# Ends of the two transformer layers of a graph network rebuilt, with four new waits on the gather queue

## The reference, cut to what matters

```python
def transformer_conv(x, edge_index, Wq, bq, Wk, bk, Wv, bv, Ws, bs):   # H = 4 heads of C = 32
    q, k, v = (x @ Wq + bq), (x @ Wk + bk), (x @ Wv + bv)              # (N, H, C)
    alpha = einsum('ehc,ehc->eh', q[dst], k[src]) / sqrt(C)
    ealpha = exp(alpha - segment_max(alpha, dst)[dst])
    attn = ealpha / segment_sum(ealpha, dst)[dst]
    out = segment_sum(attn[..., None] * v[src], dst)
    return out.reshape(N, H * C) + x @ Ws + bs

h = relu(transformer_conv(x, edges, layer 1 weights))
out = transformer_conv(h, edges, layer 2 weights)
x = layernorm(x + out)
```

## Time and profile before

| | us |
|---|---|
| runs (3) | 3877.59, 3878.28, 3880.7; median 3878.28 |
| profiled execution, its own time | 3893.77 |
| its span, first to last instruction | 3892.1 |
| busy PE / DVE / POOL / ACT | 2947.8 / 2492.3 / 2423.7 / 1048.7 |
| mean granted TensorE clock | 0.829 of 2.4 GHz |

### The profile page before, as it was taken

One profiled execution on the slowest core, in us unless ns is written; L12 is line 12 of the kernel. 1 busy time (PEld: TensorE's weight loads), 2 busy tenths in 40 slices (PEclk: granted clock), 3 DMA queues, 4 the chain that ended last, 5 costly groups with the idle time before them and its releaser, 6 DMA issues. The chain is left out here.

```text
span 3892.1 us, 57650 instructions
## 1 busy us (share of the span) xinstructions
PE 2947.8 (76%) x14303; PEld 2002.8 (51%) x14345; DVE 2492.3 (64%) x8135; ACT 1048.7 (27%) x2557; POOL 2423.7 (62%) x2427
## 2 busy tenths in 40 slices
PE   6987997746666567999977999766677776676773
PEld 3455895534444433444435777643465564364663
DVE  8886553251111377999988888873567775384876
ACT  3730664110000043333315666620011120010211
POOL 2747777647777347777754666117777734777770
PEclk8975557568888788999988999888798898888986
DMA  2222222322222147888851222026787755687872
GB/s 70 68 60 52 62 62 58 48 61 53 53 53 53 29 90 197 239 236 236 241 138 57 68 70 70 22 78 181 196 243 223 226 167 139 182 245 194 252 238 65
DMA packets 397387, 493.91 MB, mean 127 GB/s; under 512 B 64035, under 2 KB 293992, under 8 KB 397138
## 3 DMA queue, kind: packets, MB, share of 16 engines
q0 software_dynamic: 92160, 244.83, 24.3%
q1 hardware_dynamic: 304978, 245.98, 21.8%
HBM read 376.23 MB, written 114.36 MB: 126 GB/s over the span
## 5 line engine op out<-in xcount | busy, mean ns | idle before, releaser
L1918 POOL DMA_INDIRECT got<-kv_table,pair_src x832 | 839.3, 1009 | 495.4 <-issue 249.3
L686 POOL DMA_INDIRECT y_got<-y_table,y_idx x416 | 399.7, 961 | 166.2 <-issue 126.4
L1164 POOL DMA_INDIRECT got<-t_table,tile_src x392 | 378.3, 965 | 175.4 <-issue 118.8
L2167 PE MATMUL psum<-acc 125*128 x1664 | 285.1, 324 | 219.0 <-DVE h L1984 195.1
L1313 PE MATMUL sums<-msg,hot 128*125 128x260 f32 x1664 | 394.0, 390 | 31.3 <-POOL msg L1255 28.6
L2167 PEld LDWEIGHTS psum<-acc 125*128 125x128 f32 x1664 | 243.7, 224 | 297.1 <-issue 295.8
L2179 PE MATMUL psum<-h,acc 128*128 128x128 f32 x1664 | 324.0, 329 | 68.1 <-ACT hot_b L2142 37.3
L1313 PEld LDWEIGHTS sums<-msg,hot 128*125 128x125 f32 x1664 | 305.9, 189 | 119.1 <-issue 72.3
L1984 DVE TENSOR_TENSOR h<-psum,got 128x512 f32<-128x512 f32 x208 | 143.4, 690 | 348.1 <-DMA got<-kv_table,pair_src 315.1
L1255 POOL TENSOR_TENSOR msg<-rows,msg 128x512 f32<-128x512 f32 x208 | 246.3, 1204 | 188.1 <-DVE msg L1281 148.7
L628 PE MATMUL psum<-zeros 128*128 128x512 bf16 (+1 forms) x946 | 340.6, 490 | 3.5 <-issue 2.4
(11 more groups left out here) (506 smaller groups left out, 5705.3 us busy)
## 6 DMA issues: line engine op xcount, KB each, us to landing
v_rows<-got SPq DMA_DIRECT2D x208, 256.0 KB, 3.4
small<-v_rows SPq DMA_DIRECT2D x208, 256.0 KB, 4.8
dst_row<-dst_rows SPq DMA_DIRECT2D x312, 128.0 KB, 4.8
rows<-x_rows SPq DMA_DIRECT2D x104, 256.0 KB
x_rows<-small SPq DMA_DIRECT2D x104, 128.0 KB, 3.6
x_rows<-got_w SPq DMA_DIRECT2D x104, 128.0 KB, 4.5
got<-kv_table,pair_src POOLq DMA_INDIRECT x832, 3.8
y_table<-y_stage SPq DMA_DIRECT2D x25, 448.0 KB
```

The source lines that it names most:

```text
L686: pool.indirect_dma_start(out=got[:, slot, j, :], out_offset=None, in_=y_table[:, :], in_offset=bass.IndirectOffsetOnAxis(ap=m.y_idx[:, co ...
L1164: pool.indirect_dma_start(out=got[:, col % ring, :], out_offset=None, in_=table[:, :], in_offset=bass.IndirectOffsetOnAxis(ap=m.tile_src[: ...
L1918: pool.indirect_dma_start(out=got[:, slot, j, :], out_offset=None, in_=kv_table[:, :], in_offset=bass.IndirectOffsetOnAxis(ap=m.pair_src[: ...
L2167: last = t.matmul(work[:, j * P:(j + 1) * P], hot_t[:, g % 2, j // 2, j % 2, :], m.acc[:, bass.ds(ws[j], 1), 0:D].rearrange("q o d -> q (o ...
```

## The change

In `conv_layer`: the parts are added to the sums in PSUM instead of in SBUF, and the division is one product that reads PSUM and writes `m.h`, in both layers. For n = 2 the skip path is added in seven joins, the positive part is taken by ACT when it copies the transposes out, and the transposes, products and joins alternate in groups of four windows (the alternation for n = 1 too); the input x of the residual is added by PE as a product with the identity into the PSUM of the second half's products. In the last chunk the one-hots of the first two groups are made in the softmax's waits, their messages come ahead of the share arithmetic, PE runs products with zeros during that softmax (4, 3 and 24) and none behind the groups. `conv_finish` only adds the skip path and norms. POOL gets a further wait in four loops.

```diff
@@ sort_edges, POOL
             for t in range(BY_DMA):
+                if 6 * t // 5 > 8:
+                    pool.wait_ge(placed, 6 * t // 5 - 8)
@@ relation_layer, POOL
                 if g >= SL:
                     pool.wait_ge(used, g - SL + 1)
+                elif g > 2:
+                    pool.wait_ge(counted, min(4 * g - 8, groups))
@@ gat_scores, POOL
                     pool.wait_ge(scored, (g - slots) // 2 + 1)
+                    pool.wait_ge(z_done, 4 * (g - 3))
@@ conv_layer, POOL
+                if g >= 7:
+                    pool.wait_ge(q_done, g - 6)
@@ conv_layer, DVE
+            def one_hots(s):
+                if s >= 2:
+                    dve.wait_ge(summed, s - 1)
+                v.tensor_tensor(hot[:, s % 2], ..., ALU.is_equal).then_inc(hot_ready, 1)
             def messages(s):
...
-                v.tensor_tensor(hot[:, s % 2], ..., ALU.is_equal).then_inc(hot_ready, 1)
+                if s not in groups_of(last_chunk)[0:2]:
+                    one_hots(s)
@@ softmax, DVE
                 dve.sem_inc(top_ready, 1)
+                if c == last_chunk:
+                    one_hots(p0 // G)
                 dve.wait_ge(high_ready, c + 1)
...
                 dve.sem_inc(high_read, 1)
+                if c == last_chunk:
+                    one_hots(p0 // G + 1)
                 dve.wait_ge(low_ready, c + 1)
@@
-            def finish_last():
-                (reciprocal, then by four windows: product, sum with the skip path, positive part)
+            def join(k):
+                h = m.h[:, 4 * k:ends[k], :]
+                v.tensor_tensor(h, h, m.acc[:, 4 * k:ends[k], 3 * D:4 * D], ALU.add).then_inc(joined, 1)
+            if n == 2:
+                for k in range(3):
+                    join(k)
+            for k in range(TG):
+                for w in range(4 * k, ends[k]):
+                    keep_node(w)
+                if n == 2 and k + 3 < TG:
+                    join(k + 3)
+            for w in range(W):
+                keep_node(W + w)
@@
+            for s in groups_of(last_chunk)[0:2]:
+                messages(s)
             (share arithmetic)
-            for s in groups_of(last_chunk):
+            for s in groups_of(last_chunk)[2:]:
                 messages(s)
+            border = [windows(nc, m.pair_win_i, ENG.DVE, CHUNK_AT[b + 1] - 1, 1)[0] for b in range(last_chunk)]
             dve.wait_ge(shares_ready, 1)
             dve.wait_ge(closed, 1)
...
-            go(v.tensor_copy(m.h[:, :, :].rearrange("q w d -> q (w d)"), psum[0:Q, 0:W * D]))
-            (copy of the denominators, adds in SBUF, sum over three)
+            dve.wait_ge(rejoined, 1)
+            link(v.tensor_copy(part[0:Q, :, :].rearrange("q b c -> q (b c)"), work[0:Q, 0:last_chunk * (D + 3 * H)]))
+            for b, w in enumerate(border):
+                sums, ws = psum[0:Q, bass.ds(w * D, D)], psum[0:Q, bass.ds(w * 3 * H + dens, 3 * H)]
+                go(v.tensor_tensor(sums, sums, part[0:Q, b, 0:D], ALU.add))
+                link(v.tensor_tensor(ws, ws, part[0:Q, b, D:D + 3 * H], ALU.add))
+            (sum over three, maximum with 1e-30, reciprocal, all into inv)
+            v.tensor_tensor(m.h[...], psum[0:Q, 0:W * D], inv[...] over C, ALU.mult)
@@ conv_layer, ACT
-            turn_windows_act(nc, act, m, xt, tb, node_turned, node_copied)
+            for k in range(TG):
+                act.wait_ge(node_turned, k + 1)
+                nc.scalar.activation(xt[four windows], tb[k % 2][...], ACT.Copy if n == 1 else ACT.Relu).then_inc(node_copied, 1)
             for c in range(len(CHUNK)):
+                if c == last_chunk:
+                    for s in groups_of(c)[0:2]:
+                        keep(s)
                 weigh(c)
@@ conv_layer, PE
-                if c == last_chunk:
-                    for j in range(G // 2):
-                        t.matmul(psum[:, 0:512], zeros[:, 0:P], zeros[:, :], start=False, stop=False)
@@ softmax, PE
                 last.then_inc(turned, 1)
+                keep_busy(t, psum[:, 0:512], zeros, P, 4 * stay)       # stay: the last chunk
...
                 t.matmul(work[:, 0:cols], m.only127[:, :], top[:, 0:cols], start=True, stop=True).then_inc(high_ready, 1)
+                keep_busy(t, psum[:, 0:512], zeros, P, 3 * stay)
...
                 t.matmul(work[:, 0:cols], m.only0[:, :], top[:, 0:cols], start=True, stop=True).then_inc(low_ready, 1)
+                keep_busy(t, psum[:, 0:512], zeros, P, 24 * stay)
@@ conv_layer, PE, start
+            def product(k):
...
+                if half and n == 2:
+                    last = t.matmul(ob[k % 4][0:Q, D:2 * D], m.ident[0:Q, 0:Q], m.x[:, w, :], start=False, stop=True)
+            turn_nodes(0)
+            for k in range(TG):
+                if k + 1 < TG:
+                    turn_nodes(k + 1)
...
+                for w in range(4 * k, ends[k]):
+                    product(w)
+            for w in range(W):
+                product(W + w)
@@ conv_finish, DVE
-            link(v.tensor_scalar(inv[:, :, :], m.dens[:, :, :], 1e-30, None, ALU.max))
-            link(v.reciprocal(inv[:, :, :], inv[:, :, :]))
-            link(v.tensor_tensor(tmp, m.h, inv over C, ALU.mult))
-            link(v.tensor_tensor(tmp[:, :, :], tmp[:, :, :], m.acc[:, :, 3 * D:4 * D], ALU.add))
-            link(v.tensor_tensor(tmp[:, :, :], tmp[:, :, :], m.x[:, :, :], ALU.add))
+            link(v.tensor_tensor(tmp[:, :, :], m.h[:, :, :], m.acc[:, :, 3 * D:4 * D], ALU.add))
```

More of the change, by code:

```diff
@@ L1891, in conv_layer @@
         tb, ob = [psum[:, k * 512:(k + 1) * 512] for k in range(2)], [psum[:, k * 512:(k + 1) * 512] for k in range(2, 6)]
-        scaled, relued, node_turned, node_copied, node_done, node_read, kv_stored, finish_chain = (sem(x) for x in (
-            "scaled", "relued", "node_turned", "node_copied", "node_done", "node_read", "kv_stored", "finish_chain"))
+        scaled, joined, node_turned, node_copied, node_done, node_read, kv_stored = (sem(x) for x in (
+            "scaled", "joined", "node_turned", "node_copied", "node_done", "node_read", "kv_stored"))
+        ends = [min(4 * k + 4, W) for k in range(TG)]
         dens, work = W * D, psum[:, 7 * 512:8 * 512]
@@ L1990, in score @@
                     turn_hot(g + 2)
+            def one_hots(s):
+                if s >= 2:
+                    dve.wait_ge(summed, s - 1)
+                v.tensor_tensor(hot[:, s % 2],
+                                m.pair_row[:, s * G:(s + 1) * G].rearrange("l (w j) -> l w j", w=2).unsqueeze(3).broadcast_to([P, 2, 2, P]),
+                                m.iota[:, 0:P].unsqueeze(1).unsqueeze(1).broadcast_to([P, 2, 2, P]), ALU.is_equal).then_inc(hot_ready, 1)
             def messages(s):
@@ L2061, in softmax, with keep_node @@
                 dve.sem_inc(shifted, 1)
-            def finish_last():
[L2065 to L2090, removed]
+            def join(k):
+                h = m.h[:, 4 * k:ends[k], :]
+                v.tensor_tensor(h, h, m.acc[:, 4 * k:ends[k], 3 * D:4 * D], ALU.add).then_inc(joined, 1)
+            def keep_node(k):
                 half, w = divmod(k, W)
@@ L2142, in keep @@
                 nc.scalar.copy(hot_b[:, s % 2], hot[:, s % 2]).then_inc(hot_kept, 1)
-            turn_windows_act(nc, act, m, xt, tb, node_turned, node_copied)
+            for k in range(TG):
+                act.wait_ge(node_turned, k + 1)
+                nc.scalar.activation(xt[:, 4 * k:ends[k], :].rearrange("d w q -> d (w q)"), tb[k % 2][:, 0:(ends[k] - 4 * k) * Q],
+                                     ACT.Copy if n == 1 else ACT.Relu).then_inc(node_copied, 1)
             for c in range(len(CHUNK)):
+                if c == last_chunk:
+                    for s in groups_of(c)[0:2]:
+                        keep(s)
                 weigh(c)
@@ L2215, in _ @@
                     pe.wait_ge(node_read, k - 3)
-                if not half:
-                    pe.wait_ge(node_copied, w // 4 + 1)
-                t.matmul(ob[k % 4][0:Q, 0:2 * D], xt[:, w, :], w4[:, 2 * half:2 * half + 2, :].rearrange("d k c -> d (k c)"),
-                         start=True, stop=True).then_inc(node_done, 1)
+                last = t.matmul(ob[k % 4][0:Q, 0:2 * D], xt[:, w, :], w4[:, 2 * half:2 * half + 2, :].rearrange("d k c -> d (k c)"),
+                                start=True, stop=(not half or n == 1))
+                if half and n == 2:
+                    last = t.matmul(ob[k % 4][0:Q, D:2 * D], m.ident[0:Q, 0:Q], m.x[:, w, :], start=False, stop=True)
+                last.then_inc(node_done, 1)
+            turn_nodes(0)
+            for k in range(TG):
+                if k + 1 < TG:
+                    turn_nodes(k + 1)
+                else:
+                    pe.wait_ge(scaled, 1)
+                pe.wait_ge(node_copied, k + 1)
+                for w in range(4 * k, ends[k]):
+                    product(w)
+            for w in range(W):
+                product(W + w)
             pe.wait_ge(zeroed, 1)
```

41 lines of the change are left out of this document (15 added, 26 removed).

## The result

| | us |
|---|---|
| before, 6 runs | 3880.11 (3877.59 to 3880.7) |
| after, 6 runs | 3895.84 (3891.26 to 3906.33) |
| ratio | 1.0048, 95% interval 1.0035 to 1.0061 |
| profiled execution of after, its span | 3902.86, 3901.1 |
| mean granted clock | 0.832 (before 0.829) |

The changed kernel is 0.5% slower, 15.7 us, where 0.7% faster was forecast. Its runs lie 15 us apart, those of before 3.

A forecast was written before the change was run, and what follows sets the result against it. POOL's gathers were taken to bound the kernel, with chains over DVE, ACT and PE after them: 2 x (-7.6 - 1.6 + 1.2) - 6.8 - 8.1 + 4 = -26.9, giving 3851 us, range 3842 to 3864.

The forecast's parts named there:

- The clock in the last chunk: Last chunk of each layer: PE at full clock, two groups in 3.3 us, fourteen at 1.47, closing matmuls 7.6 us earlier.
- rival 1: Last chunk: without fillers PE falls to half clock, 2.8 us a group instead of 1.47; 3888 us, slower; chance 0.05.
- The wait in `gat_scores`: POOL's gather g waits for the scores' matmuls of group g-4: +4 us, ends 0 and +10.
- Rival 2: `gat_scores` becomes a closed loop, binding if data took 10.5 us; at 13 us it costs 30, 3882 us; chance 0.04.
- a sign of being wrong: The forecast is wrong if POOL's gaps in `gat_scores` sum to more than 10 us.
- The pace at full clock: Last chunk: the two-buffer loop over DVE, ACT and PE sets 1.47 us a group; lower end 1.34.
- First add 2.6 earlier: Last chunk: one-hots made in the softmax's waits and share arithmetic behind two messages bring the first add 2.6 us earlier.
- Repair and division: After the closing matmuls in each layer: reading registers ahead -1.6 us; rejoin and product out of PSUM +1.2, ends 0 and +3.
- Start of layer 2: Between the layers: joins, transposes and products alternate, -6.8 us to the fifth store, ends -8.1 and -2.
- `conv_finish`: End of the kernel: only the join is left of four passes, 11.68 to 3.55 us, -8.1.
- The other waits: POOL's new waits in edge sort, relation layer and conv layers are met at least 6 us early: 0.
- The gather pace: Both layers: POOL issues a gather every 1.25 us, 5.0 us for a group of four.

The follow-up runs named there:

- f4: Kernel before without the two products with zeros behind each group of the last chunk: 3905.69 us, ratio 1.0064.
- f1: Changed kernel with 36 instead of 24 products with zeros behind the last softmax matmul and no z_done wait in gat_scores: 3853.93 us, ratio 0.9935.
- f3: Kernel before with only the z_done wait in gat_scores added, at usual transfer speed: 3896.47 us, ratio 1.0041.
- g1: f1 also without POOL's other three new waits (edge sort, relation layer, conv layers): 3856.14 us, ratio 0.9937 to the kernel before.
- f2: Changed kernel without the z_done wait in gat_scores, at usual transfer speed: 3875.3 us, ratio 0.999 to the kernel before.
- e1: Changed kernel without the z_done wait in gat_scores, where transfers were slower: 4711.25 us, ratio 0.9588 to the kernel before.
- g3: f1 with the two products with zeros back behind each group of the last chunk: 3854.71 us, ratio 0.9935 to the kernel before.
- e2: Changed kernel with two products with zeros back behind each group of the last chunk, transfers slower: 4664.61 us, ratio 0.9479 to the kernel before.
- g2: Changed kernel with 36 products with zeros and the z_done wait looser by one group: 3856.35 us, ratio 0.9938 to the kernel before.
- e3: Changed kernel with 36 instead of 24 products with zeros behind the last softmax matmul, transfers slower: 4648.46 us, ratio 0.9456 to the kernel before.
- h1: f1 with ACT copying the one-hot twice in groups 2 to 15 of the last chunk, transfers slower: 4640.5 us, ratio 0.9513 to the kernel before.
- h2: f1 with three buffers instead of two in the last chunk, transfers slower: 4629.56 us, ratio 0.9508 to the kernel before.
- e4: Kernel before with only the z_done wait in gat_scores added, where transfers were slower: 4882.93 us, ratio 0.9935.

## Why the prediction was wrong

- **The clock in the last chunk is the step that failed first.** The forecast took two groups at 3.3 us and fourteen at 1.47 at full clock; rival 1 (half clock, 2.8 a group, chance 0.05) is what happened, at 2.56. Its guess that the fillers in the groups had kept the clock up was half of it: they had brought it back (f4), and with no standstill ahead messages keep it without them (f1). From first add to closing matmuls a layer takes 40.8 us where the sum had 23.6. It is a term of 17 us in each layer. The error was in what was compared: 57.10 busy us of 65 at a clock of 0.98 shows that messages, there mixed with scores, hold a clock that is up. I did not ask what stood directly ahead of the first add. The softmax's zeros end 5.34 us after their start, and behind them the shift, the exponential, three splittings and a message still have to be done: 2.64 us, which could have been estimated from the timelines of before. The gaps between groups (0.3 us, f1) cost the clock nothing, and it fell behind the one gap of 2.64 us. PE's load in the groups did not decide it: busy for 10.00 of 10.00 us the clock stood at 0.50, busy for 4.5 of 5 at 1.00 (f1).
- **The wait in `gat_scores`** was mis-sized: +4 with ends 0 and +10, measured +17.0 alone (f3) and +19.0 in the profile of the changed kernel. That ten of 98 gathers started ahead of the new wait was right, and so was the time of the data (median 8.9 us before, 9.05 in f3). What the replay had too small is the hand-over from PE to POOL, put at 0 to 0.3 us. In f3 no gather starts less than 0.73 us behind ACT's second one-hot instruction; in the kernel before 40 of the 98 did, not ten. With 0.73 for 0.3 the same replay, from the data times of before, gives some 11 us instead of 5 (an estimate). A gather that waits has its data later, and POOL, which paces the stage, does not make up what it lost (first to last gather 531.8 us in f3, 517.7 in f4). POOL's waits in f3:

```profile
L1537 POOL DMA_INDIRECT got_w<-wide_table,pair_src x208 | 196.8, 946 | 63.4 <-issue 49.7 <-PE z L1651 13.7
L1534 POOL DMA_INDIRECT small<-x_table,pair_src x208 | 196.4, 944 | 79.9 <-issue 58.5 <-PE got_b L1637 15.9 <-PE z L1651 5.5
```

  The clock isn't behind it: in windows of 10 us the changed kernel's stage dips twice to 0.83 (1630 and 1870), that of before once (1660). Rival 2's condition (10.5 us for data) was not needed. Its price was also wrong: by its own 0.33 us a group, 13 us for data would cost 2.5 x 0.33 x 98 = 81 us, not 30. POOL's idle time sums to 148.2 us over the two lines, before 129.6, so 18.6 more, above the 10 that were named as a sign of being wrong.
- **The pace at full clock** was mis-sized too: 1.65, not 1.47. Leaving out the zeros takes 0.43 us from PE and gives 0.3 back. With the clock held (f1) the stretch from first add to closing matmuls takes 26.2 us, where the sum had 23.6 and before shows 28.7 and 29.5 in the two layers. The loop over DVE and ACT that the sum took for the bound isn't it; PE's own 1.34, the lower end, lacked the 0.3 between groups.
- **First add 2.6 earlier**: 3.1 and 2.2 in the two layers, right. The one-hots and the zeros in the softmax did what was said.
- **Repair and division** (-1.6 and +1.2): from the closing matmuls to the product's end 11.1 us before, 10.8 in f1, right. In the changed kernel it is 12.3, for the closing matmuls run at half clock as well (3.15 us for seven of them at 0.50, in f1 1.67 at 1.00).
- **Start of layer 2** (-6.8, ends -8.1 and -2): from the first instruction (3236.07) to the first gather 22.1 us, before 31.05, so -8.95, beyond its end of -8.1. To the fifth store it is 17.8 instead of the 18.9 I had; the last us is the store's landing, 4.3 instead of 5.3. That a product of 256 columns takes 0.85 us at half clock and 0.43 at the full one holds: four take 1.73 us at 1.00 (3244.94 to 3246.67), where 24 bf16 products of 512 columns take 5.34, 0.22 each, so a column of fp32 takes four times as long as one of bf16.
- **`conv_finish`** (-8.1): -7.85. ACT's table load (1.28 us, at 3873.92) ends 8.66 us ahead of its first use, so it is covered. **The other waits** (0): 0, by g1.
- **The gather pace** was read as 1.25 us throughout; that is the median. Layer 1's 415 intervals take 545.5 us before, 1.31 each. The sum doesn't use it.

The pieces of the two profiles add up. `gat_scores` +19.0; between the layers -3.1 + 12.1 + 1.2 - 0.2 - 8.95 = +1.05; from the last gather to the end -2.2 + 11.0 - 8.1 = +0.7. That is +20.8, and the two executions differ by +9.1; the rest is that the profiled execution of before reached its first `gat_scores` gather at 1476.1, where f3 and f4, the same code up to there, reach it at 1468.2 and 1470.1, and 3.7 us among the conv gathers. In medians the wait's 17.0 less the 4.2 by which f2 is faster than before (not clear of noise: its interval reaches 1.0002) come near the 15.7 measured, with the fall of the clock paying back nearly all that the other steps gained.

With both repairs (f1) the pause between the layers is 79.5 us, where 80 was written. That agreement is partly luck: the last chunk gave 5.6 us instead of 7.6, and the start of layer 2 gave 9 instead of 6.8. From the last gather to the end f1 is 13.7 us shorter (84.4 against 98.1), where 17 was written and the terms sum to 16.1. The sum without the wait's 4 us, 3847, stands against 3853.93: 5.2 of the difference is the stretch of messages (26.2 against 23.6 in each layer), 2.2 came back at the start of layer 2, and what is left is within the noise of the medians.

## What to carry to other kernels

What PE did right before a burst of matmuls went with the clock of the whole burst here: 0.50 for the rest of 16 groups behind 2.64 us of standstill (changed kernel, e1), 1.00 for all 16 behind 0.05 us (f1). When a chain ahead of it is covered with dummy products, let them reach up to the first real one, and count that from the rows of the other engines. Dummy products inside the burst cost nothing that showed here (26.4 and 26.6 us in g3, 26.2 without them in f1), and in e2 and the kernel before they brought the clock from 0.50 back to 1.00, which the real ones alone had not (f4, 0.50 throughout). A wait added to the engine that paces a stage has to be loose in nearly every turn, with its hand-over counted: a mean slack of 0.7 us was not enough, and one group more made the same wait free (g2).

## What was not expected of the hardware

- PE at 10.00 of 10.00 us busy with fp32 products of 128 columns and bf16 products of 12 stayed at a granted clock of 0.50 for 40 us (f4 and the changed kernel), and the same stream at 1.00, busy for 4.5 of 5 us, kept it (f1). Two bf16 products of 512 columns behind each group brought it back within some 5 us (e2: 0.66 from 4600 to 4605, then 1.00), in the kernel before behind the first group (0.50 from 3175 to 3179, 0.97 from 3179 to 3184, then 1.00).
- Where the transfers are slower, the sign of the wait turns: alone it gave 0.9935 (4882.93 against 4912.74 us), where f3 had 1.0041. The length of `gat_scores` doesn't explain it: 730.1 us without the wait in e1, 701.8 and 709.2 with it in e2 and e3, but 712.6 and 704.7 without it in h1 and h2.
- The gain of 4 to 5.5% there lies largely in earlier stages. From e4, which lacks the waits in the edge sort and the relation layer, to e2, which has them, the first gather of the relation layer moves from 345.7 to 261.0 us and that layer's gathers from 733.4 to 661.4 us, together 157 of 218 us. What in the waits makes this difference no run shows; at the usual speed the same waits were worth nothing (g1). f and h ran on the same chip number, so nothing here shows that the slower transfers belong to a chip.
